# The quantised feed-forward layer of a four-layer decoder: preparation moved between the attention heads, element-wise steps dealt out anew among four engines

## What is computed

```python
def _act_quant(x):
    scale = 127.0 / jnp.clip(jnp.max(jnp.abs(x), axis=-1, keepdims=True), EPS)
    q = jnp.round(jnp.clip(x * scale, -128.0, 127.0)) / scale
    return x + jax.lax.stop_gradient(q - x)

def _weight_quant(w):
    scale = 1.0 / jnp.clip(jnp.mean(jnp.abs(w)), EPS)
    q = jnp.round(jnp.clip(w * scale, -1.0, 1.0)) / scale
    return w + jax.lax.stop_gradient(q - w)

def _bitlinear(x, w):
    xq = _act_quant(_rmsnorm(x))
    wq = _weight_quant(w)
    return jnp.einsum('bsi,oi->bso', xq, wq)

gate = jax.nn.silu(_bitlinear(x, w_gate))
up = _bitlinear(x, w_up)
return _bitlinear(gate * up, w_down)
```

## Time and profile before

| | us |
|---|---|
| median of three runs (range) | 1594.97 (1588.06 to 1594.99) |
| the profiled execution | 1592.06 |
| its span in the trace | 1589.6 |
| PE matmul busy | 1409.4 (89%) |
| DVE busy | 987.5 (62%) |
| ACT busy | 730.8 (46%) |
| POOL busy | 433.1 (27%) |
| mean granted TensorE clock | 0.94 of full |

### The profile page before, as it was taken

One profiled execution on the slowest core, in us unless ns is written; L12 is line 12 of the kernel. 1 busy time (PEld: TensorE's weight loads), 2 busy tenths in 40 slices (PEclk: granted clock), 3 DMA queues, 4 the chain that ended last, 5 costly groups with the idle time before them and its releaser, 6 DMA issues.

```text
span 1589.6 us, 25738 instructions
## 1 busy us (share of the span) xinstructions
PE 1409.4 (89%) x9822; PEld 887.5 (56%) x9840; DVE 987.5 (62%) x1782; ACT 730.8 (46%) x1747; POOL 433.1 (27%) x385
## 2 busy tenths in 40 slices
PE   7869999998899789999999988988975888988888
PEld 3535555554466456665666854755652545555636
DVE  6784323224588567777775876937778676674641
ACT  3452111112777455655664546358756453352230
POOL 3230000000000387777770000110291135224100
PEclk9979999998999989999999989999997889988899
DMA  7020311003000300000001000020010100000000
GB/s 247 27 80 1 93 31 31 0 0 159 1 2 2 120 7 7 8 7 7 8 1 74 1 22 0 1 79 2 2 45 25 54 1 2 2 1 2 28 0 27
DMA packets 21804, 48.10 MB, mean 30 GB/s; under 512 B 1458, under 2 KB 16947, under 8 KB 20532
## 3 DMA queue, kind: packets, MB, share of 16 engines
q1 hardware_dynamic: 21684, 46.47, 8.4%
HBM read 41.22 MB, written 5.24 MB: 29 GB/s over the span
## 4 chain that ended last, share of the span: by engine, by line
PE 59%; DVE 21%; ACT 7%; POOL 7%; issue 5%; DMA 0%; DVEq 0%; ACTq 0%; POOLq 0%
PE PS L748 43%; PE PS L962 5%; DVE work L2299 5%; PE PS L827 3%; PE PS L1269 2%; PE PS L1023 2%; DVE small L1849 2%; ACT work L1540 2%; PE PS L760 2%; POOL WB L621 1%; POOL WB L620 1%; POOL work L627 1%; POOL work L624 1%; PE PS L1298 1%; DVE work L1994 1%
## 5 line engine op out<-in xcount | busy, mean ns | idle before, releaser
L748 PE MATMUL PS<-XT,WB 128*128 128x512 f32 (+1 forms) x688 | 301.9, 601 | 8.6 <-issue 5.4
L748 PEld LDWEIGHTS PS<-XT,WB 128*128 128x128 f32 (+1 forms) x688 | 127.2, 192 | 153.0 <-issue 150.8
L1540 ACT ACTIVATE work<-PS,small 128x128 f32<-128x128 f32 x512 | 138.0, 419 | 48.2 <-DVE small L2099 48.2
L2069 DVE TENSOR_TENSOR work<-PS,work 128x512 f32<-128x512 f32 x48 | 33.1, 691 | 168.0 <-PE PS L748 168.0
L571 POOL TENSOR_SCALAR small<-small 128x4 f32<-128x4 f32 x22 | 5.0, 229 | 423.9 <-DVE small L1852 423.9
L1496 ACT ACTIVATE work<-PS 128x512 f32<-128x512 f32 x48 | 28.7, 597 | 193.6 <-PE PS L748 193.6
L2099 DVE TENSOR_REDUCE small<-PS 128x4 f32<-128x512 f32 x128 | 80.6, 684 | 44.2 <-PE PS L748 44.0
L748 PE MATMUL PS<-XT,WA 128*128 128x512 f32 (+2 forms) x224 | 101.4, 630 | 6.9 <-ACT XT L1403 3.3
L2299 DVE SCALAR_TENSOR_TENSOR work<-PS,vec,work 128x508 f32<-128x508 f32 (+2 forms) x108 | 80.2, 742 | 17.9 <-ACT work L1667 8.6
L962 PE MATMUL PS<-WB,work 128*128 128x256 f32 x384 | 86.6, 379 | 0.0
L748 PE MATMUL PS<-WA,XT 128*128 128x256 f32 (+1 forms) x384 | 79.9, 368 | 3.8 <-DVE XT L2119 3.0
(11 more groups left out here) (365 smaller groups left out, 2951.5 us busy)
## 6 DMA issues: line engine op xcount, KB each, us to landing
WB<-in_l0f SPq DMA_DIRECT2D x8, 768.0 KB, 7.7
WB<-in_l1x SPq DMA_DIRECT2D x1, 6144.0 KB, 17.5
WB<-in_l0f SPq DMA_DIRECT2D x32, 96.0 KB, 7.2
WB<-in_l2f SPq DMA_DIRECT2D x1, 3072.0 KB, 10.5
WA<-in_l3a SPq DMA_DIRECT2D x1, 2624.0 KB, 9.0
WB<-in_l3f SPq DMA_DIRECT2D x1, 2064.0 KB, 7.6
WA<-in_l1f SPq DMA_DIRECT2D x1, 2056.0 KB, 11.3
C<-in_ctx SPq DMA_DIRECT2D x2, 1024.0 KB, 7.1
```

Source lines behind the costliest of these rows:

```text
L748: mm = lambda o, l, r, s, e: nc.tensor.matmul(o, l, r, start=s, stop=e)
L1540: f(wk(12288 + (u % 8) * G + h * P, P), bank(j)[:, h * P:(h + 1) * P], ACT.Exp, bias=sm(704 + (u % 8) * 4 + h, 1)).then_inc(*act_step(*([j ...
L2069: v.tensor_tensor(l0f_h(m)[:, lo:lo + G], bank(j), l0f_s(m)[:, lo:lo + G], ALU.mult).then_inc(*dve_step(j))
```

## The change

- Order of jobs: the `ws` job moves from behind round 14 to behind round 7, and ACT's three sums of weights from units 20, 26, 32 to units 3, 9, 15. The two `qt` jobs of half 0 move into the heads, between the last `pv` and the last `o`; those of half 1 move behind block 2 of `gate` and `up` (`quantised_order`).
- Half 0 of the input is prepared within the heads: roots on DVE ahead of unit 54, normalising on ACT (new, four instructions), maximum and scales on DVE ahead of unit 57, scaling and MAGIC on DVE ahead of unit 60, subtraction of MAGIC on ACT (new) ahead of unit 63. It is kept in C.
- Half 1: roots behind DVE's products of block 0, normalising on ACT behind the gates of block 0, maximum, scales, scaling and subtraction on DVE behind the products of block 1. DVE takes the maxima of blocks 0 and 1 after that.
- Hidden half: scaling and MAGIC move from DVE to POOL (four blocks after each set of scales), subtraction of MAGIC from DVE to ACT (`whole`). The evictions of `ht` are shared: even blocks ACT, odd blocks DVE, which adds the residual of two blocks after each of its evictions. The scales of blocks 0 to 3 are made behind block 5 and no longer behind block 4.
- One memset of a single column at the start of DVE's program.

The core of the diff:

```diff
-SUMS_AT = 14
+QUANT_AT = (54, 57, 60, 63)
+SUMS_AT = 7
@@
+        if sums_at is not None and r == ROUNDS + 1:
+            l += [("qt", 0, 0), ("qt", 0, 1)]
@@
+def quantised_order():
+    l = [("in", b) for b in range(3)] + [("qt", 1)] + [("in", b) for b in range(3, NB)]
+    for b in range(NB + 1):
+        if b < NB:
+            l += [("ht", b)]
+        if b >= 1:
+            l += [("o", b - 1)]
+    return l
@@ gpsimd
+                pool.wait_ge(hidden_scales.sem, hidden_scales.next())
+                for b in range(4 * g, 4 * g + 4):
+                    hb = wk(b * 1024, 1024)
+                    nc.gpsimd.tensor_scalar(hb, hb, sm(168 + b, 1), MAGIC, ALU.mult, ALU.add).then_inc(scaled_hidden.sem, scaled_hidden.give())
@@ scalar
+            def input_norm(g):
+                act.wait_ge(input_roots.sem, input_roots.next())
+                for i in range(4):
+                    b = 4 * g + i
+                    f(l2f_normed(g)[:, i * D:(i + 1) * D], X[:, b * D:(b + 1) * D], ACT.Identity,
+                      bias=sm(80 + b, 1), scale=sm(88 + b, 1)).then_inc(*act_step(*([input_normed] if i == 3 else [])))
+            def input_whole(g):
+                act.wait_ge(scaled_input.sem, scaled_input.next())
+                f(l2f_whole(g), l2f_normed(g), ACT.Identity, bias=less_magic).then_inc(*act_step(whole_input))
+                    if layer == "l2x" and key[0] == "s" and key[1] == QUANT_AT[0]:
+                        input_norm(0)
+                    if layer == "l2x" and key[0] == "s" and key[1] == QUANT_AT[3]:
+                        input_whole(0)
-                    if layer == "l2x" and key[0] == "s" and key[1] in (20, 26, 32):
+                    if layer == "l2x" and key[0] == "s" and key[1] in (3, 9, 15):
...
+            def whole(b):
+                act.wait_ge(scaled_hidden.sem, scaled_hidden.next())
+                f(wkb(14336, 8192)[:, b * 1024:(b + 1) * 1024], wk(b * 1024, 1024), ACT.Identity, bias=less_magic).then_inc(*act_step(whole_hidden))
+            for b in range(NB):
+                gates(b)
+                if b == 0:
+                    input_norm(1)
+                if b == 2:
+                    quantised_evac("l2f", 1)
+                if b >= 1:
+                    squares(b - 1)
+            squares(NB - 1)
+            whole(0)
+            whole(1)
+            for b in range(2, NB + 2):
+                if b < NB:
+                    whole(b)
+                if b % 2 == 0:
+                    hidden_evac(b - 2)
@@ vector
+            products(0)
+            quantise_input(1, 0)
+            products(1)
+            quantise_input(1, 1)
+            quantise_input(1, 2)
+            v.tensor_scalar(l2f_whole(1), l2f_normed(1), MAGIC, None, ALU.subtract).then_inc(*dve_step(whole_input))
+            maxima(0)
+            maxima(1)
+            for b in range(2, NB):
+                products(b)
+                maxima(b)
+                if b == 5:
+                    hidden_factors(0)
+            hidden_factors(1)
             for b in range(NB):
-                if b == 4:
-                    activation_scales(1)
-                    dequant(1, 200, 2)
-                    dve.wait_ge(*dve_last())
-                hb = wk(b * 1024, 1024)
-                v.tensor_scalar(hb, hb, sm(168 + b, 1), MAGIC, ALU.mult, ALU.add).then_inc(*dve_step())
-                dve.wait_ge(*dve_last())
-                v.tensor_scalar(wkb(14336, 8192)[:, b * 1024:(b + 1) * 1024], hb, MAGIC, None, ALU.subtract).then_inc(*dve_step(dve_to_pe))
-                dve.wait_ge(*dve_last())
-            for b in range(NB):
+                if b % 2 == 0:
+                    hidden_evac(b + 1)
                 scaled_residual("l2f", b, 200)
```

More of the change, by code:

```diff
@@ L120, in plans @@
     p["l2x"] = ln + [(k, c, g) for c in range(2) for g in range(2) for k in ("q", "k")] + [("v",), ("mask", 0), ("mask", 1)] + heads_plan(SUMS_AT)
[L121 to L127, removed]
+    l = []
+    for what, b in quantised_order():
+        if what == "in":
+            l += [(k, b, h) for h in range(2) for k in ("gate", "up")]
+        else:
+            l += [("qt", 1, 0), ("qt", 1, 1)] if what == "qt" else [(what, b)]
     p["l2f"] = l
@@ L1195, in _ @@
             heads("l2x", w2("o"), masks)
[L1198 to L1206, removed]
-            pe.wait_ge(weights_ready, 9)
-            for b in range(NB):
[L1209 to L1219, removed]
+            pe.wait_ge(weights_ready, 9)
+            for what, b in quantised_order():
+                if what == "qt":
+                    quantised_transposes("l2f", 1)
+                if what == "in":
+                    g, t = b // 4, b % 4 * P
+                    for h in range(2):
+                        for i, n in enumerate(("gate", "up")):
+                            o = begin("l2f", n, b, h)
+                            for c in range(2):
+                                pe.wait_ge(*freed(J("l2f" if g else "l2x", "qt", g, c)))
+                                ins = mm(o, l2f_xt(g)[:, c * G + t:c * G + t + P],
+                                         wq[:, i * 2048 + c * 1024 + h * G:i * 2048 + c * 1024 + (h + 1) * G], c == 0, c == 1)
+                            end(ins)
+                if what == "ht":
+                    pe.wait_ge(whole_hidden.sem, whole_hidden.next())
                     o = begin("l2f", "ht", b).bitcast(BF16)
@@ L1732, in _, with gates @@
             heads("l2x")
[L1735 to L1746, removed]
+            def gates(b):
                 for h in range(2):
@@ new lines, in products @@
+            def products(b):
+                for h in range(2):
+                    dve.wait_ge(act_to_dve.sem, act_to_dve.next())
+                    j = J("l2f", "up", b, h)
+                    dve.wait_ge(*full(j))
+                    v.scalar_tensor_tensor(wk(b * 1024 + h * G, G), bank(j), sm(192 + b, 1), wk(10240 + h * G, G),
+                                           ALU.mult, ALU.mult).then_inc(*dve_step(j))
+                dve.wait_ge(*dve_last())
+                dve.sem_inc(dve_to_act.sem, dve_to_act.give())
@@ L2090, in heads @@
             def heads(layer):
                 for key in heads_plan(SUMS_AT if layer == "l2x" else None):
+                    if key[0] == "qt":
+                        continue
                     if key[0] == "s":
                         u = key[1]
+                        if layer == "l2x" and u in QUANT_AT:
+                            quantise_input(0, QUANT_AT.index(u))
                         j = J(layer, "s", u)
```

144 lines of the change are left out of this document (88 added, 56 removed).

## The result

Twenty runs of each kernel: 1594.98 us before (1587.52 to 1602.10), 1586.16 us after (1581.75 to 1590.74). The ratio is 0.9946, with a 95% interval of 0.9933 to 0.9959. The interval makes that a gain of 6.5 to 10.7 us, 8.8 by the medians; I forecast 6.3 from the median (1588.7, put down as 1588), so the direction and the range held and the likeliest case, a gain just inside 0.5%, was a little small.

A forecast was written before the change was run, and what follows sets the result against it. One long dependent chain on one core bounds the kernel, with PE setting the pace in the heads. Heads +2.3 and layer -8.6 give -6.3 us, from the 1594.97 median to 1588.7, forecast as 1588; range 1580 to 1598.

The forecast's parts named there:

- Heads: Heads of l2x: moved sums and preparation of half 0 make them 2.3 us longer, bounds 0.5 and 5.
- The placement of the sums: Heads: ACT's weight sums moved to rounds 1, 3, 5 cost 4.7 us against 4.35, so nothing, bounds -1 and +2.
- The preparation: Heads, rounds 18 to 21: preparing half 0 of the input adds 2.8 us, of which 2.3 remain.
- 8 us of cover for POOL's roots: Heads: POOL's weight rounding ends near 1151 us, some 8 us before DVE needs the roots ahead of unit 54.
- Part 2: Gates and products of l2f: last square 31.9 us behind the heads instead of 40.0, so 8.1 us gained.
- Part 3: Hidden half of l2f: last statistic 53 us behind the heads instead of 61.6, so 8.6 us gained.
- POOL at 1.05 a block: Hidden half: POOL's scaling takes 1.05 us a block, upper bound 2.7, done before ACT wants the blocks.
- Half clock through the hidden half: Rival, chance 0.12: PE stays at half clock there, 2.9 us a block, so the layer gains 1.6 us; 1596.
- Rounds 7 to 14 longer: Rival in the heads, chance 0.10: the early ws job holds a PSUM bank, costing 7.7 us; 1596.
- POOL the bound: Rival in the hidden half, chance 0.04: POOL's scaling takes 3.6 us a block and sets the end; 1597.
- POOL late: Rival in the heads, chance 0.02: DVE waits for POOL at unit 54; a 4 us wait gives 1593.
- The larger gain: Rival, chance 0.14: heads absorb work in waits, eviction costs 0.7; 1586, or 1583 with ACT's gate-block wait filled.

The follow-up runs named there:

- e2: The kernel before with only the three weight sums and the ws job moved early; 1600.99 us in one execution.
- e6: The changed kernel with half 0 of the input prepared right behind the heads instead of within them; ratio 1.0038 to the kernel before.
- e5: The changed kernel with the weight sums and the ws job moved back to their late places; 1617.82 us in one execution.
- e7: The changed kernel with ACT's normalising of half 1 behind the gates of block 1 instead of block 0; 1584.85 us in one execution.
- e1: The kernel before, unchanged, profiled once more; 1605.09 us.
- e8: The changed kernel with 34 matmuls added in PE's idle time ahead of the hidden half; 1582.12 us in one execution.
- e9: The changed kernel with half 1 normalised behind block 1's gates and 34 matmuls added ahead of the hidden half; 1580.95 us, ratio 0.9907 to before.

## Why the prediction held, and where it was off

- *Heads, +2.3 (bounds 0.5 and 5).* +2.4. The placement of the sums at nothing: +0.1 (e2). The preparation: 119.6 against 117.5 without it (e6), 2.1. I had summed 2.8 and given 0.5 back behind 1180 us; the rows show less added and nothing given back. From the maxima of round 18 to those of round 19 DVE takes 5.33 us and not 3.91, from there to round 20 7.41 and not 6.78: 2.1 together. So the term came out by two errors that offset each other, which is luck. As forecast, the four passes in round 20 find no idle time on DVE: they end at 1173.37 and the maxima start at 1173.40, where they followed the residual's statistics directly in the earlier trace rows.
- *8 us of cover for POOL's roots.* 1159.40 - 1151.34 = 8.1. e5 shows the price without it: 29 us.
- *Part 2, first Silu 0.65, one wait of 3 us on ACT, last square 31.9.* 0.46, 3.00 and 31.9. This part held in its mechanism too. What it did not say is that 2.8 us of DVE's own idle time stand in the chain that ACT waits for; e7 takes 1.6 us out of it.
- *Part 3, last statistic 53.* 50.8: this term was mis-sized by 2.2 us, and with it the sum (-8.6 forecast, -10.8 measured). Up to `o` 1 it is right: the first `o` starts at 36.2 (36.15 forecast), `o` 1 ends at 40.7 (40.95 by my 2.9 us a block). Then two sizes were off. The larger is PE's clock: `o` 2, which I had at half clock up to 43.9, ran at full clock and ended at 1230.44, E' + 42.3, so 1.6 us of the 2.2 are there by then. The other is the eviction of 1024 bf16 columns out of PSUM on DVE: I took 1.22 us between bounds of 0.69 and 1.3, and it took 0.66 to 0.69, the lower bound. Behind `o` 2 two blocks took DVE 3.0 us and not 3.3, and from the end of `o` 2 to the last statistic it was 8.5 us and not 9.1, 0.6 less. I had set aside the one source that had the eviction right, the Trainium skill ("VectorE: DVE Perf Modes", Why PSUM operands drop a tier), two 16-bit columns a cycle; this trace agrees with it, at 0.69 us. My own sentence put its worth at 1 us. The shares are read from the rows; no run changed the eviction alone. How early the clock rises also differs between executions (`o` 1 from 1.15 to 1.92 us), so this part could not be forecast from one profile to better than 0.8 us.
- *POOL at 1.05 a block.* 1.1 (4.42 for four). The second of its inner roots took 1.01 us now that DVE makes no passes over SBUF beside it, against 1.45 in the earlier trace rows and in e1.
- *Rivals.* Half clock through the hidden half: `o` 0 and 1 took 1.9, from `o` 2 on 1.04, so no; but its beginning costs 2.1 us (e8). Rounds 7 to 14 longer: no, they kept their pace. POOL the bound: no; its first four blocks were scaled 1.3 us before ACT took the first. POOL late: only in e5. The larger gain is the case that came closest, with 1586, for half of its reasons: the evictions were cheap, but the heads took the work at full price, and the clock, which it leaves as it was, gave most of the rest. That its number is the measured median is luck.
- *Chances.* 0.58 stood on a change within 8 us either way and 0.35 on a larger gain; the measured 8.8 lies across that line by 0.8 us.

## What to carry to other kernels

Where one engine prepares an input between two phases, look for waits of the same engine in the phase before it: here 11.5 us of delay ahead of the first gate (12.0 in e6, 0.5 in the changed kernel) turned into 2.1 us of longer heads, and without that move nothing was left of the gain. A step that is moved forward brings its suppliers along: the weight sums, worth nothing alone, had to move as well, or DVE would have stood 27.7 us behind GpSimd's queue. And when two profiles differ by less than the medians do, compare the stretch that was touched: the untouched tail of this kernel moved by 10 us between two executions of the same code. Even the touched stretch has a spread of its own (1.7 us before, 0.8 us in the hidden half), so effects of under 1 us are read together with the clock in their rows.

## What the runs showed that I had not expected

- DVE copies 1024 bf16 columns out of PSUM in 0.66 to 0.69 us, no longer than 512 f32 columns (0.69).
- The tail behind l2f, 3360 matmuls of the same kernel, took 341.4 and 351.6 us in two executions, with a mean granted clock of 0.88 and 0.85.
- 34 added matmuls in idle time shortened the layer by 2.1 us in e8, with the clock at 1.00 through it. In e9, with the same 34 and an idle time that began 1.6 us nearer to the heads, the clock was 0.79 in the stretch behind them and they shortened it by 0.3.
- The same instructions from the last square to the last statistic took 18.1 to 18.8 us in six profiled executions, by how soon the granted clock rose from 0.50 to 1.00.
